# GpSimd's drain left out at the end of every block of an eight-layer graph network kernel

## The chip, the cores and the metric

The kernel runs on one core of one Trainium2 chip. A core has five engines with a queue of instructions each: TensorE (PE), VectorE (DVE), ScalarE (ACT), GpSimd (POOL) and SyncE (SP). SP and GpSimd issue nearly all transfers: SP plain ones, GpSimd mostly indirect ones, whose addresses come from a list of indices. The metric is the time of one execution in microseconds (us), as the median of some runs.

## The reference, cut to what matters

Eight layers work on node rows `x` of 3125 nodes by 256 features: four graph layers, which gather a row for each of 50000 edges and sum them by destination, and four expert layers, which route each row to one or two of 4 to 16 small networks.

```python
    x = x + _L2_gnn_ref(_layernorm(x, axis=-1), L2_gnn_W, L2_gnn_a, src, dst)
    x = x + _L2_ffn_ref(_layernorm(x, axis=-1)[None], L2_ffn_gate_w, L2_ffn_gate_b, L2_ffn_w1, L2_ffn_b1, L2_ffn_w2, L2_ffn_b2)[0]
    x = x + _L3_gnn_ref(_layernorm(x, axis=-1), edge_index, edge_weight, edge_attr_50, L3_gnn_mlp_w1, L3_gnn_mlp_b1, L3_gnn_mlp_w2, L3_gnn_mlp_b2, L3_gnn_lin1_w, L3_gnn_lin2_w, L3_gnn_lin2_b, L3_gnn_lin_w, L3_gnn_lin_b)
    x = x + _L3_ffn_ref(_layernorm(x, axis=-1)[None], L3_ffn_router_w1, L3_ffn_router_b1, L3_ffn_router_w2, L3_ffn_router_b2, L3_ffn_expert_w1, L3_ffn_expert_b1, L3_ffn_expert_w2, L3_ffn_expert_b2, L3_ffn_expert_w3, L3_ffn_expert_b3)[0]
    return x
```

Between these lines stand a selective scan over the nodes in the order of their degree and an attention over a small graph. None of that arithmetic is touched.

## The kernel before, in words

The program is a chain of 39 stages. A stage (class `Stage`, lines 42 to 75) allocates on-chip buffers and semaphores; inside it one block holds the instructions of each engine, written out by hand with semaphore waits between the engines. 35 of the stages have a block of their own; four only hold buffers and semaphores around other stages. `Stage.block` (line 74) opens the block, and 35 places call it, counted as they run.

The end of a stage is made of three pieces, and the change touches the first.

1. The end of the block, recorded at the line that opened it (for example line 1940). All engines meet. In the program as built, each of PE, DVE, ACT and SP has a DRAIN, which waits until its engine is idle and then raises a shared semaphore, and GpSimd has a plain DRAIN. GpSimd then waits for the count of four, and releases the four others.
2. `clear_and_free_semaphores`, line 57, on GpSimd alone: a DRAIN of another kind, which carries the range of the stage's semaphores and is called the reset drain here, and EVENT_SEMAPHORE_RANGE_CLEAR, which sets them to zero.
3. `all_engine_barrier`, line 58: a second meeting, with the same instructions as the first.

Blocks in which GpSimd issues transfers end, on GpSimd, with waits for the semaphores of those transfers where they write to memory, and so with the data landed. These blocks and their lines:

- line 166, the opening: 391 scatters `rec<-rec,slot_i` (line 253), one per 128 edges;
- line 583, `edge_sums`, run three times: 416 gathers `msg` (line 607) each;
- line 844, the attention and the scan's inputs: 416 gathers `msg` (line 888) and 25 gathers `got` (line 878);
- line 1940, `block_experts`, run four times: gathers `rows<-tokens` (line 2122) and stores `answered<-y` (lines 2137 and 2142), one each for a block of tokens;
- line 1653, `fetch_pairs` when it also sorts: 25 scatters (line 1671); line 1757, `fetch_rows`: 25 gathers (line 1764);
- line 2900, the scan: 25 scatters `d_sorted` (line 2922);
- line 3097, the small graph: 256 gathers (line 3120).

In the other 22 blocks GpSimd has some memory sets, iotas and elementwise work, or nothing. In `edge_sums` and its like GpSimd runs ahead: when it has issued its last gather, PE, ACT and DVE still have rows to sum. In `block_experts` it is the reverse: the last instructions are GpSimd's stores and its waits for them.

Of the kernel before, what the change touches and what calls it, by code (L numbers as in the profile page):

```python
# [42 lines left out]
class Stage:  # L43
# [28 lines left out]
        return s  # L72

    def block(self):
        return self.nc.Block()


class Chain:
# [3519 lines left out]
```

## Time and profile before

| | |
|---|---|
| median of 3 runs | 5551.18 us |
| lowest and highest of the 3 | 5540.38 and 5554.88 us |
| span of the profiled execution | 6173.2 us |
| the profiled execution's own time | not given beyond its span |
| TensorE, granted clock (mean) | 0.802 |
| busy PE, DVE, ACT, POOL | 66%, 53%, 45%, 50% of the span |
| software DMA queue (GpSimd's) | 139600 packets, 337.72 MB |

The profile is of one execution, and its instructions have their times there. The span runs from the first to the last instruction. Drains, semaphore instructions and branches are not counted as busy; they are seen when one asks for the instructions of a line. Such rows carry a q behind the engine's name, as POOLq or PEldq (the latter is TensorE's queue). An instruction's record begins when its waits are met, and a DRAIN's record covers its wait for its own engine.

### The profile page before, as it was taken

The page shows a single profiled execution, that of the slowest core. Times are in us where ns is not written, and L with a number is a line of the kernel's source. Part 1 is how long each engine was busy: PE and PEld are TensorE (multiplying, and loading weights), DVE is VectorE, ACT ScalarE, POOL GpSimd, SP SyncE. Part 2 cuts the span into 40 slices and gives each one's busy share as a digit, 9 for nine tenths or more (in the row PEclk, how much of TensorE's full clock was granted, in tenths as well). Part 3 has the DMA queues.
Part 4 walks back from the last instruction along what each step waited for, and adds up shares of the span by engine and source line. Part 5 has one row for each costly group of instructions (what it writes and reads, how often), then busy time and mean ns, then how long its engine had stood idle before and what let it go on. Part 6 is the DMA issues. An engine that isn't in the chain of part 4 may idle for free. (4 is left out here: it accounts for less than half of the span.)

```text
span 6173.2 us, 66416 instructions
## 1 busy us (share of the span) xinstructions
PE 4074.4 (66%) x17366; PEld 2897.1 (47%) x17366; DVE 3273.6 (53%) x7095; ACT 2796.0 (45%) x6254; POOL 3072.9 (50%) x3130
## 2 busy tenths in 40 slices
PE   7888555567837777256485776857776774555665
PEld 4555333347824445222264444835555662223465
DVE  6444355456555566699634665255556125444532
ACT  4777333322335566466343442335553213666532
POOL 3666566633446566267414552436662323666333
PEclk8999777768957887699796887967776886777888
DMA  4444533355643333355502223543333324566356
GB/s 129 150 150 148 114 90 91 90 124 180 174 115 91 94 96 95 72 167 166 135 1 61 47 43 104 179 118 95 95 95 70 118 63 129 179 181 181 81 159 203
DMA packets 442553, 721.00 MB, mean 117 GB/s; under 512 B 150695, under 2 KB 322521, under 8 KB 437660
## 3 DMA queue, kind: packets, MB, share of 16 engines
q1 hardware_dynamic: 299057, 374.14, 21.6%
q0 software_dynamic: 139600, 337.72, 20.1%
q10 hardware_dynamic: 3530, 4.89, 0.2%
q8 instruction: 152, 2.49, 0.2%
q14 instruction: 214, 1.75, 0.1%
HBM read 565.71 MB, written 153.73 MB: 117 GB/s over the span
## 5 line engine op out<-in xcount | busy, mean ns | idle before, releaser
L631 PE MATMUL ps<-msg,same 128*125 128x256 f32 (+1 forms) x2496 | 953.6, 524 | 671.2 <-issue 269.6
L631 PEld LDWEIGHTS ps<-msg,same 128*125 128x125 f32 x2496 | 566.1, 251 | 986.6 <-issue 574.2
L888 POOL DMA_INDIRECT msg<-d_gat,src_i x416 | 406.0, 976 | 266.9 <-PE ps L949 137.8
L253 POOL DMA_INDIRECT rec<-rec,slot_i x391 | 379.7, 971 | 304.4 <-DVE rec L431 133.6
L607 POOL DMA_INDIRECT msg<-d_lin,src_i x416 | 393.2, 945 | 275.0 <-issue 101.9
L607 POOL DMA_INDIRECT msg<-rel_rows,src_rel x416 | 399.0, 959 | 223.1 <-issue 95.4
L607 POOL DMA_INDIRECT msg<-d_gat,src_i x416 | 393.5, 946 | 226.3 <-PE ps L631 90.7
L949 PE MATMUL ps<-msg,same 128*125 128x260 f32 x832 | 300.5, 495 | 175.9 <-DVE agg_c L1111 130.9
L278 PE MATMUL ps_f<-w,hs 128*128 128x256 f32 x1568 | 383.6, 398 | 48.9 <-DVE rec L431 30.4
L278 PEld LDWEIGHTS ps_f<-w,hs 128*128 128x128 f32 x1568 | 298.8, 196 | 156.9 <-issue 61.3
L2962 PE MATMUL ps_y<-pr,ident 128*128 128x447 f32 (+1 forms) x448 | 209.3, 593 | 238.3 <-DVE pr L3044 238.3
L2032 ACT ACTIVATE hid<-ps_h,w 128x128 f32<-128x128 f32 x572 | 207.4, 367 | 325.9 <-PE ps_h L1983 206.1
L3120 POOL DMA_INDIRECT msg<-d_small,idx x256 | 241.8, 945 | 162.6 <-DVE weighed L3223 88.7
L1983 PE MATMUL ps_h<-xT,w 128*128 128x128 f32 x2288 | 292.0, 280 | 11.3 <-DMA w<-in_L_ffn_packed 8.4
L3137 PE MATMUL ps<-spread,oh_lo 128*125 128x500 f32 x512 | 255.1, 658 | 66.8 <-DVE spread L3229 66.8
L1983 PEld LDWEIGHTS ps_h<-xT,w 128*128 128x128 f32 x2288 | 284.1, 196 | 21.4 <-DMA w<-in_L_ffn_packed 9.2
L949 PEld LDWEIGHTS ps<-msg,same 128*125 128x125 f32 x832 | 176.1, 234 | 251.2 <-DVE agg_c L1111 163.1
L2930 POOL TENSOR_TENSOR dB<-rows,u 128x894 f32<-128x894 f32 (+1 forms) x112 | 215.1, 1922 | 153.9 <-DMA rows<-bc_d 145.8
L775 DVE TENSOR_TENSOR x<-x,ps 125x256 f32 x416 | 174.7, 420 | 216.8 <-DMA w_rel<-in_w_rel 95.2
L775 DVE TENSOR_TENSOR agg_m<-agg_m,ps 125x256 f32 x416 | 174.7, 420 | 211.3 <-DMA got<-answered,slot_i 128.5
L775 DVE TENSOR_TENSOR agg_j<-agg_j,ps 125x264 f32 x416 | 178.1, 428 | 188.3 <-PE ps L631 87.9
L713 ACT ACTIVATE same<-off,cut,minus_cut 128x125 f32<-128x125 f32 x416 | 170.4, 481 | 226.7 <-DMA got<-answered,slot_i 164.0
(632 smaller groups left out, 9885.5 us busy)
## 6 DMA issues: line engine op xcount, KB each, us to landing
w<-in_L_ffn_packed SPq DMA_DIRECT2D x170, 514.0 KB
fil<-rec SPq DMA_DIRECT2D x104, 512.0 KB
rows<-bc_d SPq DMA_DIRECT2D x96, 447.0 KB
rel_rows<-row SPq DMA_DIRECT2D x25, 896.0 KB
got<-answered SPq DMA_DIRECT2D x30, 560.0 KB
ahead<-in_L_ffn_packed SPq DMA_DIRECT2D x8, 2052.0 KB
lo_rows<-ffn_lo_r SPq DMA_DIRECT2D x32, 500.0 KB
msg<-d_gat,src_i POOLq DMA_INDIRECT x832
```

What stands on the lines that cost most here:

```text
L253: nc.gpsimd.indirect_dma_start(k.rec, bass.IndirectOffsetOnAxis(slot_i[0:some_rows, c:c + 1], 0), rec[0:some_rows, g % R, j, :], None).the ...
L278: ins = nc.tensor.matmul(ps_f[:, v % 2, i, :], hs[:, (2 * g + c) % 4, j * 128:(j + 1) * 128], w2[:, c, :], start=c == 0, stop=c == 1)
L607: nc.gpsimd.indirect_dma_start(msg[:, g % R, j, :], None, table, bass.IndirectOffsetOnAxis(idx[:, n:n + 1], 0)).then_inc(msg_in[g % R], 16)
L631: nc.tensor.matmul(ps[:, j, 0:width], same[:, g % 2, j, :], msg[:, g % R, j, 0:width], start=True, stop=True).then_inc(mm, 1)
L775: nc.vector.tensor_tensor(into, into, ps[:, j, 0:width], ALU.add).then_inc(added, 1)
L888: nc.gpsimd.indirect_dma_start(msg[:, g % R, j, :], None, table, bass.IndirectOffsetOnAxis(idx[:, n:n + 1], 0)).then_inc(msg_in[g % R], 16)
L949: nc.tensor.matmul(ps[:, n % 3, 0:width], same[:, g % 2, j, :], msg[:, g % R, j, 0:width], start=True, stop=True).then_inc(mm, 1)
L1983: ins = nc.tensor.matmul(ps_h[:, at % 4, 0:BR], part(n, c * x.f + f * 128, 128), xT[:, n % 2, c, :], start=c == 0, stop=c == 1)
L2930: ins = nc.gpsimd.tensor_tensor(into, both(rows[:, n % R, 0, 0:hi - lo], hi - lo), u[:, :, lo:hi], ALU.mult)
L2962: ins = nc.tensor.matmul(ps_y[:, h, 0:size(n)], k.ident[:], pr[:, n % 2, h * size(n):(h + 1) * size(n)], start=st == 0, stop=st == SN - 1)
L3120: nc.gpsimd.indirect_dma_start(msg[:, g % R, j, :], None, table, bass.IndirectOffsetOnAxis(idx[:, n:n + 1], 0)).then_inc(msg_in[g % R], 16)
L3137: nc.tensor.matmul(ps[:, 0:NT * W], oh_lo[:, g % 2, j, :], spread[:, g % 2, j, :], start=False, stop=False).then_inc(mm, 1)
```

## The change

The block of every stage is opened with `no_gpsimd_drain=True`.

```diff
     def block(self):
-        return self.nc.Block()
+        return self.nc.Block(no_gpsimd_drain=True)
```

In the program as built this does two things in piece 1 of each of the 35 block ends. GpSimd's DRAIN is gone: after its last instruction it goes to the wait for the count of four. On PE, DVE, ACT and SP the DRAIN that raised the shared semaphore becomes a plain DRAIN and, behind it, an EVENT_SEMAPHORE that raises it. That is 35 DRAINs fewer on GpSimd (79 instead of 114) and 35 EVENT_SEMAPHOREs more on each of the four others. Pieces 2 and 3 stay as they are, with the reset drain of line 57 and the plain GpSimd DRAIN of line 58. No other instruction is added, removed or moved on any engine.

## Rows read from the trace of the kernel before

**Rows 1.** First lines of the page: the span, busy time by engine.

```profile
span 6173.2 us, 66416 instructions
```

**Rows 2.** Line 58, second meeting: durations in ns min/median/max, first and last start.

```profile
L58 POOLq DRAIN  x39: 34/34/52, 700.9 to 6173.0; - x39
...
L58 PEldq EVENT_SEMAPHORE  x39: 51/51/51, 701.1 to 6173.2; - x39
```

**Rows 3.** Line 57, the reset drain and the clear of semaphores behind it.

```profile
L57 POOLq DRAIN  x39: 49/83/203, 700.3 to 6172.8; - x39
L57 POOLq EVENT_SEMAPHORE_RANGE_CLEAR  x39: 44/110/350, 700.5 to 6172.9; - x39
```

**Rows 4.** Line 1940, end of the block, fourth run (6115 to 6136 us).

```profile
L1940 DVEq DRAIN  x1: 436/436/436, 6121.5 to 6121.5; - x1
L1940 POOLq COMPARE_BRANCH  x1: 37/37/37, 6124.8 to 6124.8; - x1
L1940 POOLq DRAIN  x1: 8879/8879/8879, 6125.0 to 6125.0; - x1
```

**Rows 5.** Line 1940, its other three runs (1680, 3990 and 5045 us on).

```profile
L1940 POOLq DRAIN  x1: 2103/2103/2103, 1684.1 to 1684.1; - x1
...
L1940 POOLq DRAIN  x1: 8552/8552/8552, 4000.8 to 4000.8; - x1
...
L1940 POOLq DRAIN  x1: 2833/2833/2833, 5053.0 to 5053.0; - x1
```

**Rows 6.** Line 166, end of the opening's block.

```profile
L166 SPq DRAIN  x1: 1014/1014/1014, 687.9 to 687.9; - x1
L166 POOLq COMPARE_BRANCH  x1: 44/44/44, 693.4 to 693.4; - x1
L166 POOLq DRAIN  x1: 6515/6515/6515, 693.6 to 693.6; - x1
```

**Rows 7.** Line 2900, end of the scan's block.

```profile
L2900 ACTq DRAIN  x1: 626/626/626, 3001.8 to 3001.8; - x1
...
L2900 POOLq DRAIN  x1: 2103/2103/2103, 3008.5 to 3008.5; - x1
```

**Rows 8.** Stretch in the drain of rows 4: five engines' busy time, clock, DMA share, GB/s.

```profile
6125.10:6133.90 8.80, 0.00 (x0) 0.00 (x0) 0.00 (x0) 0.00 (x0) 0.00 (x0) 0.50 0.00 0
```

**Rows 9.** GpSimd's transfers by line, in the stretches before the drains above.

```profile
L2137 POOL DMA_INDIRECT answered<-y,to_i x54 | 53.7, 994 | 79.7 <-DVE y L2070 65.4 <-issue 14.3
L2122 POOL DMA_INDIRECT rows<-tokens,token_i x54 | 51.9, 961 | 43.8 <-POOLq L58 27.6 <-issue 11.6 <-DVE y L2070 3.7
...
L2137 POOL DMA_INDIRECT answered<-y,to_ii x52 | 51.8, 996 | 86.5 <-DVE y L2070 84.7 <-issue 1.8
L2122 POOL DMA_INDIRECT rows<-tokens,token_ii x52 | 50.5, 971 | 42.5 <-POOLq L58 26.9 <-issue 15.6
...
L2922 POOL DMA_INDIRECT d_sorted<-kept,order_i x25 | 30.3, 1213 | 16.9 <-ACT kept L2996 11.1 <-issue 5.8
...
L253 POOL DMA_INDIRECT rec<-rec,slot_i x391 | 379.7, 971 | 304.4 <-DVE rec L431 133.6 <-issue 93.7 <-DVE slot_i L507 77.0
```

**Rows 10.** Line 1653, end of its first block (1730 to 1747 us).

```profile
L1653 POOLq DRAIN  x1: 2101/2101/2101, 1732.6 to 1732.6; - x1
...
L1653 DVEq DRAIN  x1: 1525/1525/1525, 1744.3 to 1744.3; - x1
```

**Rows 11.** Lines 583, 844, 3097 and 1757, GpSimd's drain at the end of the block.

```profile
L583 POOLq DRAIN  x3: 7344/9137/12449, 1312.8 to 5763.4; - x3
...
L583 DVEq DRAIN  x3: 434/438/469, 1335.1 to 5789.5; - x3
...
L844 POOLq DRAIN  x1: 7667/7667/7667, 2503.4 to 2503.4; - x1
...
L3097 POOLq DRAIN  x1: 16909/16909/16909, 3686.9 to 3686.9; - x1
...
L1757 POOLq DRAIN  x1: 11347/11347/11347, 5090.9 to 5090.9; - x1
```

## Prediction, as written before the result

> **What bounds the kernel now.** I read the page first, then the instructions of lines 58 and 57, then those of each line that opens a block, since the change lives at the block ends alone. The page shows the size of the thing: a span of 6173.2 us [rows 1] against a median of 5551.18 us without a profile, so the profiled execution is 11% longer than the ones that are timed. No engine is busy for more than 66% of it. The kernel is a chain of stages with a full stop after each, and what an end of a block costs is on the path of all engines, whoever bounds the stage. The reader should see in line 58's rows that a meeting of the engines is cheap as such: GpSimd's drain takes 34 to 52 ns there and the release 17 to 51 ns [rows 2]. The reset drain and the clear are small too, 83 and 110 ns in the median [rows 3].
>
> The drains at the block ends are another matter. At the end of the fourth expert block VectorE is idle by 6121.9 us, GpSimd's last wait for its transfers is met at 6124.8 us, and its drain then runs from 6125.0 for **8.88 us** [rows 4]. In that stretch no engine computes and no transfer moves: the DMA share is 0.00 [rows 8]. So the drain isn't waiting for data. The same shows in the three other expert blocks with 2.10, 8.55 and 2.83 us [rows 5], in the opening with 6.52 us [rows 6] and in the scan with 2.10 us [rows 7].
>
> What sets its length? The count of the transfers that GpSimd issued in the block. 25 scatters give 2.103 us in the scan [rows 7] and 25 again 2.101 us at line 1653 [rows 10]; 52 gathers and 52 stores, 104 together, give 8.552 us [rows 5, 9]; 54 and 54, 108, give 8.879 us [rows 4, 9]. From 104 to 108 that is 82 ns each, and from 25 to 104 it is (8552 - 2103) / 79 = 82 ns each, with 62 ns left over. A line through two points hits the others, so GpSimd's drain **walks a list of its own transfers, 82 ns an entry**, long after they have landed. The opening fits with a shorter list: 391 scatters [rows 9] but 6.515 us [rows 6], which is 79 entries, and the first expert block has 2.103 us, 25 entries [rows 5], after more than 100 transfers. Part of a long list has left it before the end; no row shows when.
>
> **Which drains are on the path.** Six of them: at line 1940 four times, at lines 166 and 2900. There GpSimd comes last even without its drain. In the opening SP's drain ends at 688.9 us and GpSimd's last branch at 693.4 [rows 6]; in the scan ACT is idle by 3002.4 us and GpSimd begins its drain at 3008.5 [rows 7]; in the expert block the gap is 2.9 us [rows 4]. In seven more blocks with transfers GpSimd's drain is hidden: at line 1653 it ends at 1734.7 us while VectorE's own ends at 1745.8 [rows 10], and in the third run of line 583 it starts at 5763.4 us, takes at most 12.4 us and so is over by 5775.9, where VectorE ends at 5789.9 [rows 11]. These seven cost nothing today. Their records also hold the last transfer's own time, so they bound the walk from above only. In the other 22 blocks GpSimd has issued nothing since the last drain and is idle early; I cost their drains at nothing, and the cover is the work of the other engines, which the change leaves where it is.
>
> **The change, part by part.**
> - Removed from the path: 6.515 + 2.103 + 8.552 + 2.833 + 8.879 + 2.103 = **31.0 us**.
> - Added on the other engines: one semaphore instruction behind the drain of whoever comes last, in the 29 blocks where that isn't GpSimd. Between the cheapest and the dearest row it is 17 to 51 ns [rows 2]; I take 50, which makes 1.5 us (bounds 0.5 and 1.5).
> - Moved: the list. It is still full when the reset drain of line 57 runs, and this is the unknown that decides. Today that drain always finds an empty list, with 49 to 203 ns [rows 3]. From below, it throws the list away at no cost. From above, it walks the list as the plain drain does, which puts all 31.0 us back and more (the first rival). [...] I take its dearest row once more for each of the 13 blocks with transfers, 13 x 0.2 = 2.6 us, the row nearest to a reset that has something to do.
> - Line 58's meeting finds an empty list as today: nothing.
>
> The sum is -31.0 + 1.5 + 2.6 = **-26.9 us**. Against the profiled span that is 6146 us, or -0.44%. The timed runs are shorter than the profile by a tenth. If the walk, which is work of GpSimd's own queue, takes the same there, the median goes to 5524; if it shrinks with the rest, -24 us and 5527. I say 5525.
>
> [...]
>
> **The rivals.**
> - **The reset drain, or line 58's, walks the list** (slower). Then the six keep their cost, and the seven hidden ones come out into the open, since their walk now starts after the meeting instead of 14 us before it. Line 1653 pays 2.1 us [rows 10] and line 1757, also with 25 transfers, as much. The five long blocks (416, 416, 416, 441 and 256 transfers) pay between 2.1 and 8.9 us each; the opening's 6.5, for 391 transfers, is nearest. That is 4.2 + 5 x 6.5 + 1.5 = +38 us, 5589. With the lowest price it is 7 x 2.1 + 1.5 = +16. [...] It decides by its price per entry: all 13 walks in the open cost 31.0 + 4.2 + 32.5 = 67.7 us at 82 ns, against 29.5 us that are saved, so from 29.5 / 67.7 = 0.44 of the present price on the change is slower.
> - **A reset of a full list has one fixed price**, the smallest loaded drain's 2.1 us. Then 13 x 2.1 = 27.3 us stand against 31.0, and with 1.5 the change is worth -2: 5549. No row speaks for it but the 2.1 us that come three times, and these are explained by 25 entries. [...]
> - **The drain waits for a moment, not for work.** If an entry only becomes free some us after its transfer, the wait goes to line 58 and all that is won is the overlap with the release, the reset and the clear, some 0.4 us in six places: -2 + 1.5, 5550. Against it: the drain takes 2.103, 2.101 and 2.103 us at three places with different work ahead of it [rows 5, 7, 10].
> - **The walk is a matter of the profile.** The profiled execution is 622 us longer, and if the walk is part of that, the timed runs have nothing to win: 5552.
>
> **How the numbers follow.** The list thrown away: 0.76. Walked: 0.08. Fixed price: 0.06. A moment, or a matter of the profile: 0.10. About 0.3%, 16.7 us, is what a measurement of this kernel can tell from no change. The first case is faster but for its edge (0.73 of 0.76), the second is slower or, at its low price, the same (0.07 and 0.01), the rest is the same. So faster 0.73, same 0.20, slower 0.07. The range: the likeliest case alone reaches from -31 + 0.5 to -24 + 4, with some 7 us for the spread of the runs shown (5540 to 5555): 5510 to 5538. Up to 5549 it takes in the fixed price, and leaves out the walk and what ends at no change.
>
> **What would show it.** In the profile after, line 1940 and its like have no POOLq DRAIN, and GpSimd's semaphore wait starts within 0.2 us of its last branch. Line 57's drain stays under 0.5 us everywhere and line 58's under 0.1. Right is that; the theory falls if line 57 or 58 shows maxima of 2 to 9 us (a walk), or 2.1 us in 13 places (a fixed price). If the profile shows the drains gone and the timed runs don't move, it was the profile's.

## The result, and the profile after

The changed kernel takes **5518.15 us** (median of 6 runs, 5508.31 to 5526.70) against 5545.03 us for the kernel before (6 runs, 5535.20 to 5554.88). That is 26.9 us between the medians. The ratio is 0.9948, with a 95% interval of 0.9935 to 0.9962, or 29 us (21 to 36). The forecast was 5525 us, from a gain of 26.9 us taken from the 5551.18 us then at hand.

First the end of the fourth run of line 1940 in the profile after, where rows 4 show a drain of 8.88 us (per row: count, duration in ns min/median/max, first and last start in us).

```profile
L1940 POOLq EVENT_SEMAPHORE  x2: 17/17/17, 5483.2 to 5483.3; - x2
...
L1940 DVEq DRAIN  x1: 448/448/448, 5479.7 to 5479.7; - x1
L1940 POOLq COMPARE_BRANCH  x1: 33/33/33, 5483.1 to 5483.1; - x1
```

GpSimd's last branch is at 5483.1 and the meeting is complete at 5483.2. VectorE had been idle since 5480.1, so GpSimd is still the last to come, 3 us after it, as in [rows 4]; only the walk is gone. The opening and the scan read alike, against [rows 6, 7]:

```profile
L166 POOLq EVENT_SEMAPHORE  x2: 17/17/17, 608.7 to 608.8; - x2
...
L166 POOLq COMPARE_BRANCH  x1: 44/44/44, 608.5 to 608.5; - x1
...
L2900 POOLq EVENT_SEMAPHORE  x2: 17/17/17, 2688.4 to 2688.5; - x2
...
L2900 POOLq COMPARE_BRANCH  x1: 41/41/41, 2688.2 to 2688.2; - x1
```

The records of this end show the edit as built. ACT's at line 166, before and then after:

```profile
L166 ACTq DRAIN  x1: 1626/1626/1626, 680.7 to 680.7; - x1
...
L166 ACTq EVENT_SEMAPHORE  x1: 17/17/17, 700.3 to 700.3; - x1
```

```profile
L166 ACTq EVENT_SEMAPHORE  x2: 17/17/17, 599.0 to 608.8; - x2
...
L166 ACTq DRAIN  x1: 1627/1627/1627, 597.4 to 597.4; - x1
```

In the first trace it is the drain's record that raises the shared semaphore; in the second it is that of the first semaphore instruction, which starts at 599.0 us, 38 ns behind the drain's end. At the first end of line 583 GpSimd issues its last gather at 1140.7 us, and its wait for the four has a record of 17 ns at 1154.0, right behind ACT's signal at 1153.9: the time before that isn't in the record. Over the whole profile GpSimd has 79 drains after 114, and ACT has 1922 semaphore instructions after 1887, 35 more; PE, DVE and SP have 35 more each as well. All instructions together are 66521 after 66416, and 4 x 35 - 35 is the difference of 105. A drain's record ends behind its engine's last work: in the scan of before, ACT's ends at 3002.41 us [rows 7] and its last ACTIVATE at 3002.37.

Did the walk move on? These are the next two pieces of the stage end, lines 57 and 58, which answer to [rows 2, 3].

```profile
L57 POOLq DRAIN  x39: 50/72/152, 608.8 to 5521.9; - x39
L57 POOLq EVENT_SEMAPHORE_RANGE_CLEAR  x39: 44/110/350, 609.0 to 5522.0; - x39
...
L58 POOLq DRAIN  x39: 40/40/188, 609.4 to 5522.1; - x39
```

It did not. The reset drain comes upon a list with entries in 13 stages now (a plain drain put in front of it takes 2.09 to 8.88 us there, under "Every walk in the open"), and its longest record is 152 ns. That record is the opening's, and it was 152 ns there before too, with the list already walked. In the other 12 of these stages the reset takes 72 to 98 ns, where it took 86 to 115 in the kernel before. The 203 ns of before stand at a stage without transfers of its own, behind the first expert block. The clears have the same 44, 110 and 350 ns as before. So the list costs neither the reset nor the clear anything.

The plain drain of line 58 behind them finds nothing to walk: 40 ns in the median, 188 at most. That one record is over the 0.1 us that the prediction had set as a limit for line 58. It stands at 4200.0 us, at the end of the second of line 2449's stages, in which GpSimd issued no transfer, so it isn't a walk; at the 13 stages with transfers line 58's drain takes 40 to 57 ns. The list is thrown away, at no price. Whether the reset drain or the clear behind it does this, no run separates, since one always follows the other; "the reset" stands for both below.

| | before | after |
|---|---|---|
| median | 5545.03 us | 5518.15 us |
| span of the profiled execution | 6173.2 us | 5522.3 us |
| GpSimd drains at block ends, on the path | 31.0 us | none |
| reset drain, median and longest | 83, 203 ns | 72, 152 ns |
| line 58's GpSimd drain, median and longest | 34, 52 ns | 40, 188 ns |

The two spans are not to be compared: the profiled execution of before moved its data more slowly (117 GB/s over its span against 131), and it is 11% longer than the timed ones. A second profile of that kernel, below, has a span of 5537.0 us.

### The profile page after: what moved, and what is told of

It is laid out like the page before. It is cut to its first block and busy times, and to the rows that moved or that the text cites. A ratio compares the mean times of both kernels' runs of the same rounds, so it can differ in the third digit from the quotient of the medians.

```text
span 5522.3 us, 66521 instructions
## 1 busy us (share of the span) xinstructions
PE 3965.1 (72%) x17366; PEld 2884.1 (52%) x17366; DVE 3284.4 (59%) x7095; ACT 2800.9 (51%) x6254; POOL 3067.6 (56%) x3130
## 5 line engine op out<-in xcount | busy, mean ns | idle before, releaser
L631 PEld LDWEIGHTS ps<-msg,same 128*125 128x125 f32 x2496 | 584.9, 256 | 807.5 <-DVE msg L764 266.7
L278 PE MATMUL ps_f<-w,hs 128*128 128x256 f32 x1568 | 366.6, 387 | 8.4 <-DVE hs L422 8.0
L949 PE MATMUL ps<-msg,same 128*125 128x260 f32 x832 | 285.1, 481 | 83.6 <-DVE agg_c L1111 83.2
L2930 POOL TENSOR_TENSOR dB<-rows,u 128x894 f32<-128x894 f32 (+1 forms) x112 | 215.2, 1922 | 154.6 <-DMA rows<-bc_d 150.4
L2070 DVE TENSOR_TENSOR y<-ps_o,b 128x256 f32<-128x256 f32 (+1 forms) x202 | 85.7, 424 | 312.2 <-PE ps_o L2008 242.6
L2962 PEld LDWEIGHTS ps_y<-pr,ident 128*128 128x128 f32 x448 | 81.7, 201 | 359.8 <-DVE pr L3044 211.6
L2058 DVE COPY xT<-ps_t 128x256 f32<-128x256 f32 (+1 forms) x186 | 83.0, 446 | 308.1 <-PE ps_t L1969 305.0
L422 DVE SCALAR_TENSOR_TENSOR hs<-ps_h,minus_b,hid 128x512 f32<-128x512 f32 x196 | 146.6, 749 | 195.7 <-ACT hid L357 195.0
L703 ACT ACTIVATE off<-ramp_r,minus_lo 128x125 f32<-128x125 f32 x832 | 260.3, 384 | 2.4 <-PEq L58 2.4
```

The source lines that it names most:

```text
L278: ins = nc.tensor.matmul(ps_f[:, v % 2, i, :], hs[:, (2 * g + c) % 4, j * 128:(j + 1) * 128], w2[:, c, :], start=c == 0, stop=c == 1)
L631: nc.tensor.matmul(ps[:, j, 0:width], same[:, g % 2, j, :], msg[:, g % R, j, 0:width], start=True, stop=True).then_inc(mm, 1)
L703: ins = nc.scalar.activation(off[:, b, j, :], k.ramp_r1[:], ACT.Abs, bias=k.minus_lo1[:, n:n + 1])
L949: nc.tensor.matmul(ps[:, n % 3, 0:width], same[:, g % 2, j, :], msg[:, g % R, j, 0:width], start=True, stop=True).then_inc(mm, 1)
L2930: ins = nc.gpsimd.tensor_tensor(into, both(rows[:, n % R, 0, 0:hi - lo], hi - lo), u[:, :, lo:hi], ALU.mult)
L2962: ins = nc.tensor.matmul(ps_y[:, h, 0:size(n)], k.ident[:], pr[:, n % 2, h * size(n):(h + 1) * size(n)], start=st == 0, stop=st == SN - 1)
```

## The experiments

All were run against the kernel before, in three groups with one chip each. Ratios are to that kernel in the same group, with a 95% interval.

### The kernel before again

No edit.

> The kernel before, unchanged, for a second profile and as a control. The first profile had a span of 6173 us against a median of 5545. Theory (the drain walks a list of GpSimd's transfers, 82 ns an entry, and that is work of its own queue): in a profile of the usual length the six drains on the path take the same as in the first, 6.5, 2.1, 2.1, 8.6, 2.8 and 8.9 us within 0.1. Rival (the walk's length is a matter of the profile): they shrink with the span, by a tenth or more. Ratio to the kernel before: 1.000 within 0.002.

Measured: 5540.81 us, ratio 0.9994 (0.9984 to 1.0004). In its profile, line 166 and the four runs of line 1940:

```profile
span 5537.0 us, 66416 instructions
...
L166 POOLq DRAIN  x1: 6515/6515/6515, 604.2 to 604.2; - x1
...
L1940 POOLq DRAIN  x1: 2103/2103/2103, 1503.0 to 1503.0; - x1
...
L1940 POOLq DRAIN  x1: 8552/8552/8552, 3578.7 to 3578.7; - x1
...
L1940 POOLq DRAIN  x1: 2833/2833/2833, 4527.9 to 4527.9; - x1
...
L1940 POOLq DRAIN  x1: 8879/8879/8879, 5489.0 to 5489.0; - x1
```

The numbers are those of [rows 4, 5, 6] to the nanosecond, in a span that is 636 us shorter. The walk takes a fixed time in GpSimd's queue, and it doesn't depend on how fast the transfers were: they moved 117 GB/s over the first span and 130 over this one. The rival that the profile had made it falls.

### The six ends alone

```diff
-    def block(self):
-        return self.nc.Block()
+    def block(self, **how):
+        return self.nc.Block(**how)
...
-        with s.block() as block:
+        with s.block(no_gpsimd_drain=True) as block:
```

The second hunk stands at lines 166, 1940 and 2900, which run six times.

> Only the six block ends at which GpSimd's loaded drain was on the path (line 166, the four runs of line 1940, line 2900) are opened without the drain; the 29 others are as before. Theory: nearly all of the gain comes from these six, -31.0 us and 6 x 0.1 or so for the reset drain, so -30 to -31 (ratio 0.9945). If the gain came from all 35 ends alike, these six would give 6/35 of 27 us, -4.6.

Measured: 5515.18 us, 0.9942 (0.9927 to 0.9956). In us of the kernel before that is -32 (-40 to -24). Within this interval the whole gain comes from six ends of 35.

### The other 29 alone

The same edit with the choice turned round.

> The complement: the 29 other block ends without the drain, the six as before. Theory: nothing to win, and one semaphore instruction more on the engine that comes last, +0.5 to +2 us (ratio 1.000 within 0.001). The seven hidden loaded drains vanish without a trace in the time. Rival (gain from all ends alike): -22 us.

Measured: 5542.59 us, 0.9995 (0.9986 to 1.0003), no change. Seven loaded drains went with these ends and the time shows nothing of it: they were hidden. The price of the extra semaphore instruction can be read from the records all the same. From the end of the last instruction of another engine that is neither a drain nor a semaphore instruction (a branch counts) to the completed meeting it takes 153 ns in the mean in the kernel before and 216 ns here, over the 29 and 28 ends where that is under 0.3 us. That is 63 ns each, 1.8 us in all, which the interval of this run (-8 to +2 us) can't resolve.

### Every walk in the open

```diff
         self.ctx.close()
+        self.nc.gpsimd.drain()

         self.nc.clear_and_free_semaphores(self.sems)
```

> The changed kernel with one plain GpSimd drain put between the first meeting and the reset drain at all 39 stage ends, so that every list is walked where nothing hides it. Theory (a walk costs by its entries, whenever it is done): the six as before, 31 us, and the seven that were hidden now in the open, 2.1 us each at lines 1653 and 1757 and 4 to 9 us each at the five long ones: +35 to +45 us against the kernel before (ratio 1.0065 to 1.008), and in the profile 13 long drains, those of the 25 transfers at 2.10 us each though the transfers landed 10 to 20 us earlier. Rival (the drain waits for a moment some us after the landing): the seven cost 0.04 us each and the total is that of the kernel before, ratio 1.000.

Measured: 5566.27 us, 1.0044 (1.0028 to 1.0059), slower by 24 us (16 to 33). The inserted drain, line 56 of that kernel, first over the whole run and then in seven of the thirteen stretches where it finds a list; between them the transfers of lines 1671 and 1764:

```profile
L56 POOLq DRAIN  x39: 34/40/8879, 609.1 to 5563.4; - x39
...
L56 POOLq DRAIN  x1: 2668/2668/2668, 1161.9 to 1161.9; - x1
...
L1671 POOL DMA_INDIRECT order_d<-ids,rank_i x25: 1182/1228/2349, 1514.2 to 1555.1; - x25
...
L56 POOLq DRAIN  x1: 2095/2095/2095, 1571.3 to 1571.3; - x1
...
L56 POOLq DRAIN  x1: 2337/2337/2337, 2223.2 to 2223.2; - x1
...
L56 POOLq DRAIN  x1: 5282/5282/5282, 3324.6 to 3324.6; - x1
...
L56 POOLq DRAIN  x1: 8552/8552/8552, 3595.0 to 3595.0; - x1
...
L56 POOLq DRAIN  x1: 2667/2667/2667, 4211.5 to 4211.5; - x1
...
L1764 POOL DMA_INDIRECT got<-answered,slot_i x25: 1191/1267/1994, 4552.9 to 4592.1; - x25
L56 POOLq DRAIN  x1: 2091/2091/2091, 4617.1 to 4617.1; - x1
```

Two things are to be seen. The last of 25 scatters was issued at 1555.1 us and the drain begins at 1571.3, 16 us later; it takes 2.095 us. At line 1764 the distance is 25 us, and it takes 2.091. In the kernel before the drain began 2.8 us after the last scatter's issue and took 2.101 [rows 10]. So time doesn't shorten a walk: the rival of the moment falls. Nor do bytes set its length: the scatters of line 1671 move one integer per row and those of line 2900's block 256 features per row, and 25 of either take 2.10 us [rows 7, 10].

The other is the size. The third run of line 583 takes 2.668 us like the first. The seven walks that used to be hidden come to 2.668 + 2.095 + 2.337 + 5.282 + 2.667 + 2.091 + 2.668 = **19.8 us**. In the records the 26 other inserted drains take 1.1 us together, the step behind each of the 39 is 27 ns, 1.1 us, and the semaphore instructions of the 29 ends are 1.8 us. That makes 23.8 us, against 24 measured. I had expected 35 to 45, since I gave the five long blocks 4 to 9 us each. The reset drains of this kernel find every list walked and take 54 to 152 ns, no less than in the changed kernel, where 13 lists had entries.

By an estimate from 62 + 82 ns an entry, the long lists hold 32 entries after 416 transfers (three times), 28 after 441 and 64 after 256. 416 - 32 is 4 x 96 and 256 - 64 is 2 x 96, as though 96 entries left at a time; but 391 - 79 = 312, 441 - 28 = 413 and the first expert block's 128 - 25 = 103 don't fit that. The third expert block doesn't either: it issues 68 transfers (32 gathers and 36 plain stores) and keeps 34, while the 104 and 108 of the second and fourth stay whole.

One pause may belong to this. In the first expert block the 114th transfer (a store of line 2137) starts 3.25 us after the instruction in front of it, where the other stores start after 0.7 to 1.1 us. This pause stands there, the same within a nanosecond, in every profile taken but that of the next experiment, with its drain halfway: there it is 0.74 us. If the list is cut at that transfer, 15 are still to come, so 10 of the 113 before it were left on it to make the 25 of the end; that is worked out, not seen. What shortens a list in one block, and not at all at 104 or 108, stays open.

### A drain halfway

On the kernel before, in line 1940's block:

```diff
                 for n in range(blocks):
...
                     pool.wait_ge(o_done, TB * (n + 1))
+                    if n == blocks // 2:
+                        pool.drain()
```

> The kernel before with one more plain GpSimd drain in the middle of line 1940's four blocks, after half of the token blocks. Theory (82 ns for every transfer issued since the last drain and still on the list): at the end of the blocks only what was issued since is left. Run 2 (104 transfers) keeps about 26 stores and 19 gathers, 45 entries, 3.7 us instead of 8.55; run 4 (108) 27 and 20, 3.9 us instead of 8.88; run 3 about 18, 1.5 us instead of 2.83; and run 1, which had 2.10 us with only 25 entries left of 128, gets longer: 32 and 25, 57 entries, 4.7 us. Rival (the drain's length belongs to the place, not to a list): the end drains stay as they are.

Measured once: 5541.77 us. The drain at the end of the block, in its four runs:

```profile
L1940 POOLq DRAIN  x1: 4710/4710/4710, 1508.5 to 1508.5; - x1
...
L1940 POOLq DRAIN  x1: 3727/3727/3727, 3589.2 to 3589.2; - x1
...
L1940 POOLq DRAIN  x1: 1521/1521/1521, 4532.3 to 4532.3; - x1
...
L1940 POOLq DRAIN  x1: 3896/3896/3896, 5496.9 to 5496.9; - x1
```

Expected were 4.7, 3.7, 1.5 and 3.9 us. The first run is the telling one: a drain more in the middle makes the drain at the end longer, 4.71 us instead of 2.10, because an estimated 57 entries are left where there had been 25 of 128. It is the count on the list that sets the length, not the place. The one time, 5541.77 us against 5540.46 for the kernel before in its group, says nothing further. The four drains at the end are 8.5 us shorter together, and the four in the middle take 4.1 to 5.9 us each; how much of these is covered by other work was not measured.

### The second meeting bare

```diff
-        self.nc.all_engine_barrier()
+        self.nc.all_engine_barrier(sem_only=True)
```

> The changed kernel, and line 58's second meeting made of semaphores alone as well, 39 times. By the theory this meeting finds an empty list, since the reset drain has thrown it away, so only GpSimd's idle drain of 40 ns and its step to the next instruction go: 39 x 0.1 = -4 us against the changed kernel at most, ratio to the kernel before 0.994 to 0.995. If line 58's drain did something dear that the trace doesn't show, the gain would be tens of us.

Measured: 5505.50 us, 0.9937 (0.9922 to 0.9953). By the two ratios that is 6 us more than the changed kernel's gain, where 4 at most were expected. But the intervals overlap (0.9935 to 0.9962 there), and the changed kernel itself reads 0.9932 in the last group below, so the times don't tell the extra gain from nothing. The records do better: from the end of the clear to the last release of the second meeting it takes 233 ns in the median instead of 297, so 2.4 us for 39 of them.

### Rare clears

```diff
-        self.nc.clear_and_free_semaphores(self.sems)
-        self.nc.all_engine_barrier()
+        self.k.spent = getattr(self.k, "spent", []) + self.sems
+        if self.must or self.nc.free_len() < 64:
+            self.k.flush()
```

`flush` clears what was put aside and lets the engines meet; `must` is set in the opening and the route stages.

> The changed kernel with the semaphores of ended stages kept aside, and cleared only when fewer than 64 are free or where GpSimd's last work has no semaphore of its own (the opening and the route stages): 12 resets, clears and second meetings instead of 39. One such piece takes 0.48 to 0.9 us in the trace from the end of the first meeting on. Theory: 27 x 0.5 = -13 to -16 us against the changed kernel, ratio to the kernel before 0.992. Its risk: GpSimd's list is no longer thrown away at each stage, so if it grows long something in the middle of a stage may have to shorten it, at a price of up to 2 to 8 us each time.

Measured: 5501.07 us, 0.9932 (0.9918 to 0.9945). The clears of this kernel (line 36):

```profile
L36 POOLq DRAIN  x12: 70/103/179, 605.4 to 5280.2; - x12
L36 POOLq EVENT_SEMAPHORE_RANGE_CLEAR  x12: 69/240/547, 605.5 to 5280.3; - x12
```

12 resets and clears instead of 39, and the clears are longer. They come in eight flushes, four of which clear two ranges, so there are only eight second meetings and not the 12 that I had counted: 31 fewer, not 27. The median is 17 us under the changed kernel's, in another group of runs; by the two ratios it is 9 us. The expected 13 to 16 lie between, and the intervals overlap. In the profiles the short stages that lost the piece are 0.3 to 0.6 us shorter, as line 1514's first, from 33.9 to 33.4 us; at some 0.45 us for 31 of them that is an estimated 14 us. From one first meeting to the next no stage is more than 2.6 us longer than in the changed kernel's profile (the scan, 392.7 us after 390.0), and the changed kernel's own second profile has 391.6 us there, so the feared 2 to 8 us are not seen.

### The six ends and rare clears

The edit of the six ends and that of the rare clears together, with `must` in the opening, the expert blocks and the scan.

> The six block ends alone without the drain (0.9942), and rare clears: 11 instead of 39, forced after the opening, the four expert blocks and the scan, where the reset throws the list away. GpSimd's plain drain stays at the 29 other ends, hidden. Theory: -30 - 28 x 0.5 = -44 us against the kernel before, ratio 0.992, and 1 to 3 us better than the same with all drains left out.

Measured: 5498.85 us, 0.9922 (0.9908 to 0.9935), -43 us against the -44 expected. The six ends alone had 0.9942 (0.9927 to 0.9956) in another group, so the two intervals overlap a little. Within its own group it is 2 us under the rare clears with all 35 drains left out (5501.07 us), as expected in sign, but less than either varies by.

### Both, with the bare meeting, beside the changed kernel

> The six block ends alone without the drain, rare clears (11), and the second meeting behind each clear made of semaphores alone. Theory: the six give 0.9942, rare clears took it to 0.9922, and 11 bare second meetings at 0.1 us are worth -1 us more: 0.992. A gain of more than 2 us from the bare meeting would say that its drains cost more than their records show.

> The changed kernel (all 35 ends without the drain) with rare clears (12) and bare second meetings. Theory: 0.9932 as with rare clears alone, less 1 us; and 2 to 4 us slower than with the drain left out at the six ends only, since the 29 others carry a semaphore instruction more each on the engine that comes last.

> The changed kernel itself, on the same chip and in the same rounds as the two combinations. 0.9948 within 0.001; the combinations should stand 0.2 to 0.3% under it.

Measured in the same rounds: the six ends with rare clears and bare meetings 5506.29 us, 0.9912 (0.9896 to 0.9928); all 35 ends with both 5504.06 us, 0.9911 (0.9896 to 0.9927); the changed kernel 5518.54 us, 0.9932 (0.9915 to 0.9950). Here the kernel before had a median of 5556.28 us, higher than in the groups before, so that the same changed kernel reads 0.9932 after 0.9948: a ratio carries some 0.15% from group to group. Within the group the combinations are 12 and 14 us under the changed kernel, or 0.22 and 0.26%, though their intervals against the kernel before overlap with its own. The bare meeting was to be judged by a gain of more than 2 us, and a ratio that moves by 8 us from group to group can't tell that. Which of the two combinations is better can't be told either; that leaving the drain at the 29 ends saves 2 to 4 us was expected and is not seen.

## Why the prediction was right

- **The drain walks a list, 82 ns an entry.** Right, and the firmest of all steps: the halfway drain gave four predicted lengths within 0.1 us. Shown is that the length follows a count; that there is a list which is walked is the picture for it. The prediction passed over one number that its line didn't hit: the third expert block's 2.833 us is 34 entries, after 68 transfers.
- **Six walks on the path, 31.0 us.** Right. The six alone give 0.9942, which is -32 us, and the 29 others 0.9995.
- **The cover of the seven hidden ones.** Right: with all 29 other ends changed the time stayed within -8 to +2 us, where the seven walks are 19.8 us long in the open.
- **The reset drain throws the list away.** Right, but no row of before showed it: there the reset always came behind a drain that had walked the list, and took 49 to 203 ns [rows 3]. That the list would be thrown away rather than walked, and with it the chance of 0.76, was my estimate. The walks in the open show that the list is there when the reset comes (13 drains of 2.09 to 8.88 us in front of it). The profile after shows that it goes, in 39 records of at most 152 ns and with nothing to walk at line 58 (40 ns in the median, 188 at most). No run shows why, nor whether it is the drain or the clear behind it.
- **The reset's price, 2.6 us.** Wrong in size: it is nothing. I had taken its dearest row for a reset with something to do, but the 203 ns stood at a stage without transfers, and at the 13 with them the reset is no longer with entries than without.
- **The semaphore instruction, 1.5 us.** Mis-sized a little. It costs 63 ns an end, 1.8 us, more than the dearest row that I had called the bound, since the step to it counts beside its own 17 to 51 ns: from the end of the drain in front it is 44 to 64 ns in the median, by engine, in the profile after.
- **The sum.** With these two terms it would have been -31.0 + 1.8 = -29.2, next to the ratio's -29 and well within its interval, -36 to -21. That the forecast's -26.9 is also the difference of the two medians is chance: it holds the 2.6 us that aren't there. Of the 7 us between 5525 and 5518, 6 are the kernel before, whose median fell from 5551 to 5545 with three more runs.
- **The range.** Its lower end doesn't follow from its own terms: 5551 - 30.5 - 7 is 5514, not 5510. The result lies inside either.
- **The same in timed runs as in the profile.** Right: the walks are equal to the nanosecond in spans of 6173 and 5537 us, so no part of them shrinks.
- **The first rival's price, +38 us.** Wrong in size, as the open walks show: 19.8 + 1.5, so +21 us. What was wrong is the price by the nearest row. The opening's 391 transfers left 79 entries, while 416 gathers leave 32. The hidden records gave no closer price, since they hold more than the walk: at line 3097 the drain's record starts at 3686.9 us, the last gather's at 3697.5, and the drain reads 16.9 us [rows 11] where the walk in the open takes 5.28. The list wasn't walked at lines 57 and 58, so the forecast didn't suffer.
- **A fixed price of 2.1 us.** Fell: no record of line 57 or 58 comes near it; the longest in the profile after are 152 and 188 ns, and 350 ns for the clear.

## What to carry to other kernels

Before a wait in front of a meeting is costed, ask whether its engine comes last, and read that from the ends of the other engines: here six of 35 drains held all of the gain. Where an instruction's length is odd, set it against a count of what was issued before it; two equal counts with equal times (25 and 25 for 2.10 us) say more than a mean over all. And where work might only move, look for the instruction behind it that would have to do it, then read exactly that row afterwards.

## What was not expected of the hardware

- A plain drain of GpSimd took 2.10 us after 25 of its own transfers, 8.55 after 104 and 8.88 after 108, which is 82 ns each and 62 ns over. It took as long well after they had landed: 2.095 and 2.091 us for 25 of them, 16 and 25 us after the last was issued, with a DMA share of 0.00 in both drains. In the fourth expert block GpSimd's last wait for its transfers was met at 6124.8 us, and the 8.88 us came after that, with a DMA share of 0.00 [rows 4, 8].
- The reset drain and the clear behind it empty the same list for nothing: in the 13 stages with entries the drain takes 72 to 152 ns in the profile after, and 86 to 152 ns in the kernel before, where the list was already walked. The clear has the same 44, 110 and 350 ns in both.
- More transfers can mean a shorter walk: it took 2.67 us after 416 gathers, 2.83 after 68 transfers and 8.88 after 108, an estimated 32, 34 and 108 entries at 82 ns. In the first expert block, whose 128 transfers leave 2.10 us, a pause of 3.25 us stands in front of the 114th. With an added drain in the middle that pause was 0.74 us and the last drain 4.71 us.
